# Three stages of a transformer-like chain sorted by expert, and their results added inside the loop's own block

## The reference, cut to what matters

```python
h_shared = _swiglu(flat @ shared_in_w.T)
out_shared = h_shared @ shared_out_w.T + shared_out_b
...
comb = jnp.zeros((S, E), flat.dtype).at[rows, disp].add(topv)
cnt = jnp.zeros((S, E), flat.dtype).at[rows, disp].add(1.0)
h_expert = _swiglu(flat @ expert_in_w.T)
routed = cnt @ expert_out_bias
for e in range(E):
    routed = routed + comb[:, e:e + 1] * (h_expert @ expert_out_weight[e].T)
```

```python
h = jax.nn.relu(jnp.einsum('td,edh->teh', xf, W1) + b1[None])
y = jnp.einsum('teh,ehd->ted', h, W2) + b2[None]
mu = jnp.mean(y, axis=-1, keepdims=True)
var = jnp.mean((y - mu) ** 2, axis=-1, keepdims=True)
y = (y - mu) / jnp.sqrt(var + EPS) * gamma[None] + beta[None]
out = jnp.sum(gate_w[:, :, None] * y_sel, axis=1)
```

## Time and profile before

| what | value |
|---|---|
| median of three runs | 3418.93 us (3418.81 to 3420.36) |
| the profiled execution | 3418.41 us |
| its span in the trace | 3416.6 us |
| mean granted clock of PE | 0.879 |
| PE busy | 2692.3 us, 79% of the span |
| DVE, ACT, POOL busy | 1641.9, 1103.5, 492.9 us |
| stage `sro` | 1249 to 1437 us of the span |
| stage `nee` | 3207.4 to 3408.6 us |

### The profile page before, as it was taken

How to read it: one execution, slowest core, us unless ns; L and a number is a source line. 1 busy time by engine, 2 the same in 40 slices (tenths; PEclk the granted TensorE clock), 3 DMA queues, 4 the chain that set the end, 5 groups by cost and what they waited for, 6 DMA issues and landing times. The chain is left out here.

```text
span 3416.6 us, 52562 instructions
## 1 busy us (share of the span) xinstructions
PE 2692.3 (79%) x18611; PEld 2115.4 (62%) x18611; DVE 1641.9 (48%) x3209; ACT 1103.5 (32%) x2099; POOL 492.9 (14%) x758
## 2 busy tenths in 40 slices
PE   6988598699777689866957888888888888735695
PEld 4867597599467444454636777777777777524453
DVE  3636321322257312333326777777777777433353
ACT  2323121122132100001105555555555555323242
POOL 0000122122021000000000111111111111100077
PEclk9989699699689699977988999999999999857797
DMA  4000122243231010112671311342343431120100
GB/s 114 1 7 1 54 88 74 75 126 110 56 87 41 25 56 0 30 22 98 237 235 53 101 60 38 105 116 70 103 136 96 132 96 31 40 50 1 41 25 25
DMA packets 122566, 243.92 MB, mean 71 GB/s; under 512 B 30040, under 2 KB 69682, under 8 KB 118480
## 3 DMA queue, kind: packets, MB, share of 16 engines
q1 hardware_dynamic: 108592, 203.06, 19.2%
q0 software_dynamic: 13728, 37.64, 4.5%
HBM read 451.99 MB, written 53.98 MB: 148 GB/s over the span
## 5 line engine op out<-in xcount | busy, mean ns | idle before, releaser
L2190 PE MATMUL tx_ring<-g_ident,tx_p 128*128 128x128 f32 x2552 | 427.6, 299 | 129.1 <-issue 46.1
L2190 PEld LDWEIGHTS tx_ring<-g_ident,tx_p 128*128 128x128 f32 x2552 | 315.6, 151 | 223.4 <-issue 63.6
L2408 DVE TENSOR_REDUCE tx_neg_max<-tx_scores 128x1 f32<-128x1354 f32 x232 | 362.3, 1562 | 46.5 <-PE tx_scores L2178 46.5
L2415 DVE COPY tx_p_t<-tx_ring 128x512 f32<-128x512 f32 x464 | 306.9, 687 | 135.8 <-PE tx_ring L2190 130.6
L2315 ACT ACTIVATE tx_p<-tx_scores,tx_neg_max 128x1354 f32<-128x1354 f32 x232 | 322.4, 1390 | 97.2 <-DVE tx_neg_max L2408 96.8
L2178 PE MATMUL tx_scores<-tx_keys,tx_queries 96*128 96x512 f32 (+1 forms) x696 | 222.2, 432 | 31.6 <-DMA tx_queries<-tx_q_hi 31.3
L2322 ACT ACTIVATE tx_p_t<-tx_ring 128x384 f32<-128x384 f32 x232 | 113.4, 489 | 356.7 <-PE tx_ring L2190 355.7
L2229 PE MATMUL tx_ring<-tx_p_t,tx_values 128*32 128x128 f32 x5104 | 151.5, 274 | 21.4 <-ACT tx_p_t L2322 20.9
L1297 PE MATMUL sro_ring<-sro_we,sr_h 128*128 128x512 f32 x352 | 155.6, 601 | 6.1 <-DMA sro_we<-_L_ffn_expert_out_weight 6.1
L2229 PEld LDWEIGHTS tx_ring<-tx_p_t,tx_values 128*32 128x32 f32 x5104 | 135.9, 110 | 35.1 <-ACT tx_p_t L2322 34.3
L2178 PEld LDWEIGHTS tx_scores<-tx_keys,tx_queries 96*128 96x128 f32 x696 | 128.1, 213 | 44.4 <-issue 32.1
(11 more groups left out here) (747 smaller groups left out, 5282.8 us busy)
## 6 DMA issues: line engine op xcount, KB each, us to landing
tx_keys<-expert_keys SPq DMA_DIRECT2D x696, 169.5 KB
lv1e_w<-in_L_ffn_W SPq DMA_DIRECT2D x232, 256.0 KB
tx_w<-in_L_ffn_W SPq DMA_DIRECT2D x58, 1024.0 KB
lv0e_w<-in_L_ffn_W SPq DMA_DIRECT2D x200, 256.0 KB
tx_values<-expert_values SPq DMA_DIRECT2D x58, 704.0 KB
tx_rows<-in_L_ffn_rows SPq DMA_DIRECT2D x29, 640.0 KB, 3.7
g_adj_t<-in_adj_t POOLq DMA_DIRECT2D x4, 3872.0 KB, 22.8
expert_values<-kv_v SPq DMA_DIRECT2D x8, 1408.0 KB, 5.7
```

What stands on the lines that cost most here:

```text
L2190: last = nc.tensor.transpose(ring[u % 2][:, (t - t0) * P:(t - t0 + 1) * P], p[n % 2][:, t * P:(t + 1) * P], g.ident[:])
L2408: nc.vector.tensor_reduce(neg_max[:, n % 4:n % 4 + 1], sc[n % 2][:, 0:N], AX_X, ALU.max, negate=True)\
L2415: nc.vector.tensor_copy(p_t[:, n % TURNED, t0:t0 + nt, :], ring[u % 2][:, 0:nt * P].rearrange("p (t q) -> p t q", q=P))\
```

## The change

What it does, part by part:

1. `ne` becomes sorted. `stage_spread` and `stage_normalised_experts` go; `stage_plan` (`nep`) comes, and `stage_normed_tiles`, a loop of 29 tiles, keeps the name `nee`. SP loads the weights of a tile's expert into one of three sets, if it isn't the expert that the set holds.
2. `sr` becomes sorted in its output part. `stage_spread` goes and a plan (`srp`) comes. `stage_gated_hidden` makes the shared half as before, and the routed half by rows: 11 blocks of four matmuls with 512 columns, each block stored to a new tensor `hidden_dram`. `stage_routed_out` is replaced by `stage_routed_tiles`: the shared output first, then 29 tiles whose hidden rows (2 KB each) are fetched, turned, and multiplied with one expert's weight.
3. `stage_combine` goes. What it did is a class `Returns`, used inside the tile loop's own block by all five sorted stages (`lv0e`, `lv1e`, `tx`, `sro`, `nee`). The load of the results waits for the `sent` semaphores only. The old value is added by POOL (`sum`), no more by PE; level 0 has none.
4. The coefficients are turned inside `stage_plan` (11 transposes and three copies). `stage_load` blanks a row of `hidden_dram` with two transfers of 1 KB more. `x` normed and its transpose share their memory with the loaded results. Weights come in other layouts from the host.

The diff, cut to its core. The queues of the new loop of `ne`:

```diff
+def stage_normed_tiles(nc, g, tag, w_dram, cols_dram, rows_dram, plan, acc, beta_dram):
...
+            for i in range(SETS, tiles):
+                sync.wait_ge(second_done, i - SETS + 1)
+                sync.wait_ge(out_done, i - SETS + 1)
+                load(i)
+            back.load(sync, sent, all_sent)
+
+        @block.gpsimd
+        def _(pool):
+            def fetch(i):
+                if i >= 3:
+                    pool.wait_ge(turned_full, i - 2)
+                fetch_rows(nc, plan, g.source_dram, xg[:, i % 3, :], i).then_inc(x_loaded[i % 3], 16)
+
+            for i in range(3):
+                fetch(i)
+            for i in range(tiles):
+                if i + 3 < tiles:
+                    fetch(i + 3)
+                pool.wait_ge(out_done, i + 1)
+                send_rows(nc, g, plan, out[:, i % 2, :], i).then_inc(sent[i % 2], 16)
...
+            back.sum(pool)
+
+        @block.tensor
+        def _(pe):
+            def turn(i):
+                pe.wait_ge(x_loaded[i % 3], 16 * (i // 3 + 1))
+                if i >= 2:
+                    pe.wait_ge(turned_read, i - 1)
...
+            turn(0)
+            turn(1)
+            first(0)
+            for i in range(tiles):
+                if i + 2 < tiles:
+                    turn(i + 2)
+                if i + 1 < tiles:
+                    first(i + 1)
+                second(i)
+            back.spread(pe, spare + wide)
...
+            for i in range(tiles):
+                if i + 2 < tiles:
+                    keep_rows(i + 2)
+                if i + 1 < tiles:
+                    hide(i + 1)
+                deviation(i)
...
+            result(0)
+            for i in range(tiles):
+                if i + 1 < tiles:
+                    result(i + 1)
+                normalise(i)
+            back.mix(dve, spare + wide)
```

The queues of the new loop of `sr`, behind its shared part:

```diff
+def stage_routed_tiles(nc, g, tag, h, shared_dram, expert_dram, plan, bias_dram):
...
+            for i in range(3):
+                fetch(i)
+            for i in range(tiles):
+                if i + 3 < tiles:
+                    fetch(i + 3)
+                pool.wait_ge(y_done, i + 1)
+                send_rows(nc, g, plan, y[:, i % 2, :], i).then_inc(sent[i % 2], 16)
...
+            turn(0)
+            for i in range(tiles):
+                if i + 1 < tiles:
+                    turn(i + 1)
+                project(i)
+            pe.wait_ge(shared_added, NB)
+            back.spread(pe, spare)
...
+            for i in range(tiles):
+                dve.wait_ge(done, i + 1)
+                if i >= 2:
+                    dve.wait_ge(sent[i % 2], 16 * (i // 2))
+                nc.vector.tensor_copy(y[:, i % 2, :], row[i % 2][:, 0:D]).then_inc(y_done, 1)
```

The stores of the routed hidden rows in `stage_gated_hidden`:

```diff
+            for b in range(NB):
+                n = rows_of(b)
+                sync.wait_ge(rows_done, b + 1)
+                sync.dma_start(g.hidden_dram[b * P:b * P + n, :], h_rows[0:n, b % 3, :]).then_inc(kept[b % 3], 16)
+            for k in range(3):
+                sync.wait_ge(kept[k], 16 * ((NB + 2 - k) // 3))
```

And `Returns`, with what it replaces:

```diff
-                last = nc.tensor.matmul(row[b % 4][:, 0:D], turned_sb[:, b * P:(b + 1) * P], table[:], start=True, stop=not add)
-                if add:
-                    last = nc.tensor.matmul(row[b % 4][:, 0:D], g.ident[:], acc[:, b, :], start=False, stop=True)
...
+    def load(self, sync, sent, counts):
+
+        full = N // P
+        for sem, count in zip(sent, counts):
+            sync.wait_ge(sem, count)
...
+    def spread(self, pe, banks):
+        pe.wait_ge(self.table_loaded, 16)
+        if self.pads:
+            pe.wait_ge(self.pads_loaded, 16)
+        for b in range(NB):
+            if b >= len(banks):
+                pe.wait_ge(self.first_done, b + 1 - len(banks))
+            self.nc.tensor.matmul(banks[b % len(banks)][:, 0:D], self.plan.coef_t[:, b * P:(b + 1) * P], self.table[:],
+                                  start=True, stop=True).then_inc(self.row_full, 1)
+
+    def mix(self, dve, banks):
+
+        for b in range(NB):
+            n = rows_of(b)
+            dve.wait_ge(self.row_full, b + 1)
+            self.there(dve, b)
+            if self.add and b >= 2:
+                dve.wait_ge(self.summed, b - 1)
...
+    def sum(self, pool):
+        for b in range(NB):
+            n = rows_of(b)
+            pool.wait_ge(self.second_done, b + 1)
+            self.nc.gpsimd.tensor_tensor(self.acc[0:n, b, :], self.acc[0:n, b, :], self.with_second[0:n, b % 2, :],
+                                         ALU.add).then_inc(self.summed, 1)
```

More of the change, by code:

```diff
@@ new lines, in _ @@
+            pe.wait_ge(w_loaded[1], 16)
+            for b in range(NB):
+                if b == 0:
+                    pe.wait_ge(gate_done, HT)
+                if b == 1:
+                    pe.wait_ge(h_done, HT)
+                if b >= 2:
+                    pe.wait_ge(row_gate_done, b - 1)
+                    pe.wait_ge(rows_done, b - 1)
+                for half in range(2):
+                    for k in range(KD):
+                        last = nc.tensor.matmul(wide[b % 2][:, half, :], src_t[:, k, b * P:(b + 1) * P],
+                                                w[1][:, k, half * HID:(half + 1) * HID], start=(k == 0), stop=(k == KD - 1))
+                last.then_inc(rows_full, 1)
@@ new lines, in _ @@
+                for f in range(HT):
+                    last = nc.tensor.matmul(spare[b % 4][:, 0:D], h[:, f, b * P:(b + 1) * P], ws[:, f, :],
+                                            start=(f == 0), stop=(f == HT - 1))
+                last.then_inc(shared_full, 1)
+            turn(0)
[5 more added lines that the diff above has]
+            back.spread(pe, spare)
@@ L1478, in _ @@
         def _(act):
+            for c, (b0, n) in enumerate(TG):
+                act.wait_ge(turned_full, c + 1)
+                nc.scalar.activation(plan.coef_t[:, b0 * P:(b0 + n) * P], turned[:, c, 0:n * P], ACT.Copy).then_inc(turned_read, 1)
             act.wait_ge(hot, 1)
@@ L1682, in stage_hidden_tiles @@
         h_act, h_dve, y_done = s.sem("h_act"), s.sem("h_dve"), s.sem("y_done")
+        back = Returns(nc, g, s, plan, acc, b2_dram, add, pads=True)
+        all_sent = [16 * ((tiles + 1 - k) // 2) for k in range(2)]
         block = ctx.enter_context(nc.Block())
@@ L1749, in _ @@
             for k in range(2):
-                pool.wait_ge(sent[k], 16 * ((tiles + 1 - k) // 2))
+                pool.wait_ge(sent[k], all_sent[k])
+            back.load_pads(pool)
+            if add:
+                back.sum(pool)
         @block.tensor
@@ L2166, in _ @@
                     load_weight(i, w2, a["L2_ffn_W2"], w2_loaded)
+            sync.wait_ge(full, at["queries", tiles - 1, 0] + 1)
+            back.load_table(sync)
+            back.load(sync, stored, [16 * ((tiles + 1 - k) // 2) for k in range(2)])
         @block.tensor
@@ L2608, in transformer_experts @@
         experts = a["L2_ffn_wq"].shape[0]
[L2609 removed]
+        plan = Plan(s, experts, experts)
         with ExitStack() as inner:
@@ new lines, in normalised_experts @@
+def normalised_experts(nc, g, a):
+    with ExitStack() as ctx:
+        s = Pool(nc, ctx, "ne")
+        experts = a["L3_ffn_Wg"].shape[1]
+        plan = Plan(s, experts, experts)
+        with ExitStack() as inner:
+            t = Pool(nc, inner, "new")
+            weights, mask = t.sb("weights", [P, NB, experts]), t.sb("mask", [P, NB, experts])
+            stage_route(nc, g, "ner", g.xn_t, a["L3_ffn_Wg"], experts, "logits", weights, mask)
+            stage_plan(nc, g, "nep", weights, mask[:], plan, coef=weights, src=g.xn)
+        stage_normed_tiles(nc, g, "nee", a["L3_ffn_w"], a["L3_ffn_cols"], a["L3_ffn_rows"], plan, g.x, a["L3_ffn_beta"])
```

671 lines of the change are left out of this document (351 added, 320 removed).

## The result

The changed kernel takes 3529.59 us (median of four runs, 3526.69 to 3531.13) beside 3418.87 us of the kernel before: slower by a ratio of 1.0326 (95% interval 1.0311 to 1.0340). The forecast was 3508 us, range 3440 to 3550: the time lies in the range, 22 us above the forecast.

What follows compares the result with a forecast made beforehand. It took the new `ne` tile loop to be bound by a serial chain at half clock, 11.8 us a tile; 3418.4 - 5 - 15 - 12.5 - 32 + 154.5 gave 3508 us, range 3440 to 3550.

Steps and rivals of the forecast that it cites:

- The chain of `ne`: Normalised experts' tile loop: fetch, PE, DVE and POOL follow one another at half clock, 11.8 us a tile; block +154.5 us.
- The weights: `ne` loop: a new expert's weights come about as late as the turned rows, hidden by a little; otherwise 1 us a tile more.
- Rivals 1 and 4: `ne` loop: 1, the chain at full clock, 3453 us, chance 0.14; 4, no chain, 3289 us, 0.09 with kin.
- The shared and routed block: Plan, hidden stage, 29 tiles at 3.1 us and returns replace spread and `sro`: 169.2 against 201.9 us, -32.
- The returns: Ends of sorted stages: earlier load, 4.9 us drain behind POOL's last add; level 0 -5, level 1 -15, transformer experts -12.5 us.

Runs made afterwards that it cites:

- the first run: Changed kernel with DVE doing normalise(i) right after result(i) in the `ne` loop: 3384.67 us, ratio 0.9899 to the kernel before.
- the filled run: Changed kernel with 24 useless 128x128 matmuls on PE after second(i) in the `ne` loop: 3496.23 us, ratio 1.0219.
- the second run: Changed kernel with six buffers of fetched rows in place of three in the `ne` loop, fetches six tiles ahead: 3493.66 us, ratio 1.0212.
- the tenth run: Changed kernel, DVE's order kept, with six row buffers, four weight sets and weight loads waiting only for the second product of i-4: 3319.13 us, ratio 0.9699.
- the open ring: Changed kernel, `ne` loop with normalise(i) after result(i), six row buffers, four weight sets and earlier weight loads: 3317.84 us, ratio 0.9701.
- seventh run: The open ring's kernel with six buffers of fetched rows and four of results in the routed loop: 3292.84 us, ratio 0.9624.
- the eighth run: The open ring's kernel with DVE, not POOL, adding the old value, before the results are there: 3289.52 us, ratio 0.9623.

## Why the prediction was right

The mechanism was right, and most of the 154.5 us rest on it; the sum came out 22 us short, 18 of them in one other term.

**The chain of `ne`** was the step that carried the sum, and its order held in each link: 11.80 us a tile where 11.8 were worked out, +156.7 us where +154.5 were. That the two agree so closely is partly luck, for two terms missed in opposite directions. Means over the 24 tiles: POOL 1.57 between `out` and fetch (forecast 1.59), the landing 4.10 (3.6), PE 4.07 (4.46), DVE 2.06 (2.17). PE's part is below half clock's 4.46 in every tile, 3.6 to 4.2. That it is a chain is shown by the first run (one link shortened, two tiles for each wait), that its PE part was the half clock by the filled run. By the Trainium skill ("TensorE: Matmul & The Clock Gate", section on HAM oscillation) such bursts between waits stay at the lower clock in every tile; the trace agrees, with 0.58.

**The weights** were said to be hidden by a little. Right in the changed kernel: once PE has turned, it goes on without a wait in all 24 tiles. Where new weights come the first product starts 4.9 us after the second weight load's issue began (3367.97 to 3372.89), and in the second run, where PE waits there, 3.9 (3332.28 to 3336.19), so 1 us is hidden. The loads were the next bound as soon as the fetches were not: the second and the tenth run.

**Rivals 1 and 4** (full clock, no chain) did not come, but both exist: the filled run comes near the first, with 10.17 a tile on average and 9.84 over the 19 tiles at full clock, where 9.6 were worked out, and the open ring is the fourth, 3.24 where 3.0 were.

**The shared and routed block** is the term that was mis-sized: -14.1 in place of -32. From the trace after, beside the forecast's own steps: the plan took 26.0 us and not 24.4 (1133.3 to 1159.3); the hidden stage 90.4 where 83.4 + 4.3 were expected, since the last rows are ready at 1243.97 and the next block opens only at 1249.7: the slowest of these stores takes 4.2 us to land, where 2.9 were allowed; the loop with its shared part 127.2 and not 114.9, since a tile took 3.48 and not 3.1; and the return 27.3 and not 25.6. Together 18. The fetch of 2 KB rows lands 5.3 us after its issue in place of 4.0, which is 0.4 a tile in a ring over three tiles, and DVE waited seven times for a send to land before it could copy:

```profile
DMA to landing us min/median/max: 3.2/5.3/7.3
```

The landing had been taken from a loop with half the bytes. Deeper buffers took the loop below the 3.1 of the forecast (seventh run).

**The returns** were right in their mechanism: early load, and the drain of 4.9 us behind POOL's last add. One size was off wherever POOL adds, 1.7 us in each such return (`tx` gave 10.7 and not 12.5, level 1 12.6 and not 15): a block takes 1.08 us and not 0.93, since DVE's second sum is 657 ns beside POOL's addition and 485 without it. No row of before had shown the two together in this form.

**What stays open:** what bounds the routed loop at 2.86 us in one kernel and 2.66 in another, differences of some 5 us between traces in loops that an edit doesn't touch, and the +3.0 us in the hyperbolic layer and the last route.

## What to carry to other kernels

Write the ring of a tile loop out as one sum: start at a fetch, follow each wait and each place in a queue until the same fetch of a later tile, and count how many tiles that takes. A buffer that is refilled behind another job's send in the same queue is no prefetch: here two swapped steps of DVE's queue turned a loss of 3.3% into a gain of 1.0%, and six row buffers with four weight sets into one of 3.0%. When one link is freed, look for the next before the run (here the weight loads behind `out`), and let the engine with the long drain finish its last work while another still has sums to do.

## What the runs showed of the hardware that was not expected

- POOL's drain at a block's end, 4.2 to 4.9 us, can lie under other engines' work: it cost nothing in level 0, and 4.9 us behind the last add of level 1. In the eighth run it began at 881.2 in level 1, under DVE's sums.
- DVE's weighted sum of 128x256 takes 485 ns alone and 656 to 657 at the median while POOL adds tiles of the same size.
- The same matmuls of the same tiles had a granted clock of 0.58 with a wait at every tile (7.6 us in the one shown), 0.76 with one at every second tile, 0.98 with the ring open, and 0.96 with useless matmuls in the waits.
